# A third row group in seven block products, and the row groups in another order

## The reference

```python
h = relu(layernorm(x))                                   # 5120 x 64
u = par_u[0] * par_u[1] * (diag_u[:, None] * h[:2048] @ W_u) + h[:2048]
i = par_i[0] * par_i[1] * (diag_i[:, None] * h[2048:] @ W_i) + h[2048:]
e = concatenate([u, i])                                  # 5120 x 64
g = adj @ (adj.T @ e)                                    # two products with the large matrix
out = x + layernorm(g) * ln_gamma + ln_beta + h
```

## Time and profile before

| what | before |
|---|---|
| median of 3 runs | 371.39 us (371.16 to 372.5) |
| the profiled execution | 371.32 us |
| its span, first to last instruction | 369.5 us |
| TensorE busy | 98% of the span |
| VectorE, GpSimd, ScalarE busy | 71%, 43%, 20% |
| mean granted TensorE clock | 0.997 of full speed |
| HBM read | 131.55 MB, 360 GB/s over the span |

### The profile page before, as it was taken

The page is one execution under the profiler, slowest core; times in us unless marked ns, Lnnn a source line. Parts: engine busy times, 40 slices in busy tenths (PEclk is TensorE's granted clock), DMA queues, the critical chain, the costliest instruction groups (busy, mean ns, idle before and its releaser), DMA issues.

```text
span 369.5 us, 10865 instructions
## 1 busy us (share of the span) xinstructions
PE 360.3 (98%) x4776; PEld 151.7 (41%) x4776; DVE 263.0 (71%) x282; ACT 74.3 (20%) x213; POOL 159.6 (43%) x94
## 2 busy tenths in 40 slices
PE   7998999999999999999999999999999999999994
PEld 4664454543323443443334334334433343344432
DVE  5999994999061969395677839694956768385266
ACT  5863022010050004001300500040023005002422
POOL 2023060020019902970793199049607931990036
PEclk9999999999999999999999999999999999999998
DMA  8999999999999978989898989889898989853933
GB/s 311 422 419 415 418 426 419 419 419 402 403 380 411 363 291 331 427 343 411 323 429 331 419 326 425 338 318 421 349 409 326 427 339 413 325 247 132 426 130 142
DMA packets 19897, 133.22 MB, mean 361 GB/s; under 512 B 2209, under 2 KB 2977, under 8 KB 4001
## 3 DMA queue, kind: packets, MB, share of 16 engines
q1 hardware_dynamic: 19440, 132.22, 88.1%
q10 hardware_dynamic: 432, 0.66, 0.5%
HBM read 131.55 MB, written 1.31 MB: 360 GB/s over the span
## 4 chain that ended last, share of the span: by engine, by line
PE 87%; DMA 7%; POOL 2%; SPq 2%; DVE 1%; issue 0%; ACT 0%; DVEq 0%; POOLq 0%
PE h_acc L887 36%; PE t_acc L918 24%; DMA natural<-adj_rows 7%; PE x_acc L955 7%; PE h_acc L975 7%; PE t_acc L856 5%; PE t_acc L955 5%; PE h_acc L870 2%; POOL xs L424 1%; SPq L289 1%; POOL sums L420 1%; PE t_acc L993 1%; DVE xs L795 0%; SPq L286 0%; DVE sums L784 0%
## 5 line engine op out<-in xcount | busy, mean ns | idle before, releaser
L599 DVE STREAM_TRANSPOSE strips<-natural 128x2048 f32<-128x2048 f32 x76 | 169.0, 2279 | 48.2 <-PE h_acc L887 48.0
L887 PE MATMUL h_acc<-strips,tokens 32*64 32x512 f32 x2432 | 133.5, 589 | 0.1
L918 PE MATMUL t_acc<-natural,e 128*32 128x512 f32 x832 | 92.3, 592 | 0.1
L887 PEld LDWEIGHTS h_acc<-strips,tokens 32*64 32x64 f32 x2432 | 53.3, 132 | 79.4 <-issue 74.3
L399 POOL TENSOR_TENSOR sums<-natural 128x1024 f32<-128x1024 f32 x14 | 33.3, 2381 | 113.4 <-DMA natural<-adj_rows 113.4
L918 PEld LDWEIGHTS t_acc<-natural,e 128*32 128x32 f32 x832 | 27.4, 110 | 59.4 <-issue 58.2
L955 PE MATMUL x_acc<-sums,forms 128*32 128x256 f32 x280 | 41.1, 380 | 0.0
L856 PE MATMUL t_acc<-natural,e 128*64 128x256 f32 x320 | 36.5, 382 | 1.4 <-DMA natural<-adj_rows 1.1
L489 ACT COPY smalls<-x_acc 32x256 f32<-32x256 f32 x7 | 2.6, 365 | 170.1 <-PE t_acc L955 170.1
L479 ACT COPY tokens<-tokens 32x384 f32<-32x384 f32 (+2 forms) x60 | 24.2, 403 | 51.6 <-DVE tokens L623 30.9
L407 POOL TENSOR_TENSOR sums<-natural,sums 128x1024 f32<-128x1024 f32 x14 | 33.3, 2379 | 1.1
(11 more groups left out here) (97 smaller groups left out, 299.8 us busy)
## 6 DMA issues: line engine op xcount, KB each, us to landing
natural<-adj_rows SPq DMA_DIRECT2D x100, 1024.0 KB, 7.9
cols<-adj_cols SPq DMA_DIRECT2D x20, 1024.0 KB, 11.6
natural<-adj_last SPq DMA_DIRECT2D x4, 1024.0 KB, 10.8
out<-xs SPq DMA_DIRECT2D x4, 256.0 KB, 2.0
xs<-x ACTq DMA_DIRECT2D x2, 256.0 KB, 5.3
xs<-x SPq DMA_DIRECT2D x2, 256.0 KB, 7.7
out<-xs SPq DMA_DIRECT2D x2, 128.0 KB, 2.0
smalls<-small SPq DMA_DIRECT2D x1, 150.0 KB, 3.6
```

The costliest lines, as they stand in the source:

```text
L599: nc.vector.transpose(strips[:, a, :, m].rearrange("p c t i -> p t c i"), natural[:, a, m].rearrange("p t (c j) -> p t c j", j=Q)).then_in ...
L887: last = nc.tensor.matmul(h_acc[D * s:D * (s + 1), q], t[part, a, b, u, :], rows, start=(isinstance(g, int) and g == 0 and b == 0 and u == 0),
L918: last = nc.tensor.matmul(t_acc[lane, pair_bank(half)].rearrange("p (a w) -> p a w", a=2), e[:, GT * m + 2 * k + s, Q * v:Q * (v + 1)], na ...
```

## The change

Row groups 4, 1 and 2 of pairs 3 to 9 are now in seven block products; 0 and 3 stay plain. `ORDER` becomes (0, 4, 1, 2, 3): `first_early` does 0 plain and 4 summed, `first_rest` does 1 and 2 summed and 3 plain. GpSimd has twelve adds for a pair in place of eight, in the order 4, 1, 2. There is no more room for the new sums, so the sums of row group 2 take the three places of those of row group 4, and one of them takes the second half of the slot of row group 4 of the even panel. That slot is therefore loaded in two halves: the first as soon as row group 4 of the pair before is multiplied, the second (semaphore `s_late`) only when row group 2 of the pair before is. The transposes of a pair are taken in another order, seven of the eight before the work on `t`; `u` and `v` move to another PSUM tile, and `v` is made before the first `turn_t`.

```diff
-ORDER = (0, 1, 4, 2, 3)
-EARLY = 2
-TURNS = (0, 1, 3, 2)
-BEHIND = 2
-SUMMED = (4, 3)
+ORDER = (0, 4, 1, 2, 3)
+TURNS = ((0, 0), (0, 1), (0, 2), (1, 0), (1, 1), (0, 3), (1, 2), (1, 3))
+BEHIND = 1
+SUMMED = (4, 1, 2)
+SHARED = 2
-SCRATCH = 2048
+SCRATCH = 1024
...
-        u, sixth_rest, _, v = (x_acc[Q * lane:Q * (lane + 1), WIDE:2 * WIDE] for lane in range(QUADRANTS))
+        sixth_rest = x_acc[Q:2 * Q, WIDE:2 * WIDE]
+        u, v = (t_acc[0:Q, 1, WIDE * n:WIDE * (n + 1)] for n in range(2))
...
+            def load_half(g, s, loaded):
+                sp.dma_start(block_of(0, TURNED, s).rearrange("p k c -> p (k c)"),
+                             adj_rows[g, TURNED, :, HALF * WIDE * s:HALF * WIDE * (s + 1)]).then_inc(loaded, 16)
...
             for g in range(PAIRED + 2, PANELS, 2):
+                sp.wait_ge(s_first, firsts_pair(g // 2 - 1, TURNED))
+                load_half(g, 0, s_natural[0][TURNED])
+                load_natural(g + 1, TURNED)
                 for a in range(2):
-                    for m in range(EARLY):
-                        refill(g + a, m)
-                for m in (4, 3, 2):
-                    for a in range(2):
-                        refill(g + a, m)
+                    refill(g + a, 0)
+                for a in range(2):
+                    refill(g + a, 1)
+                sp.wait_ge(s_first, firsts_pair(g // 2 - 1, SHARED))
+                load_half(g, 1, s_late)
+                for a in range(2):
+                    refill(g + a, 2)
+                refill(g, 3)
                 for a in range(2):
                     refill_cols(g - 2 + a)
+                refill(g + 1, 3)
...
                 for m in SUMMED:
                     for a in range(2):
                         pool.wait_ge(s_natural[a][m], 16 * (half + 1))
-                    pool.wait_ge(s_first, firsts_pair(half - 1, m))
+                    if m == SHARED:
+                        pool.wait_ge(s_first, firsts_pair(half, TURNED))
+                    else:
+                        pool.wait_ge(s_first, firsts_pair(half - 1, SHARED if m == TURNED else m))
...
+                    if m == TURNED:
+                        pool.wait_ge(s_late, 16 * (half - FIRST_HALF))
                     pool.wait_ge(s_sums, sums_done(half, m, 3))
                     nc.gpsimd.tensor_tensor(sum_of(m, 3), block_of(0, m, 1), sum_of(m, 1),
                                             ALU.subtract).then_inc(s_sums, 1)
...
+                dve.wait_ge(s_v, 2 * (half - FIRST_HALF) - 1)
+                nc.vector.tensor_tensor(v, first_v, uv, ALU.add).then_inc(s_v, 1)
                 dve.wait_ge(s_t_left, left + 3)
                 turn_t(2 * half, 0, slice(0, WIDE))
-                dve.wait_ge(s_v, 2 * (half - FIRST_HALF) - 1)
-                nc.vector.tensor_tensor(v, first_v, uv, ALU.add).then_inc(s_v, 1)
...
             def first_rest(half):
-                first_summed(half, 4)
-                first_plain(half, 2)
-                first_summed(half, 3)
+                first_summed(half, 1)
+                first_summed(half, 2)
+                first_plain(half, 3)

             def first_early(half):
-                for m in range(EARLY):
-                    first_plain(half, m)
+                first_plain(half, 0)
+                if not isinstance(half, int):
+                    pe.wait_ge(s_v, 2 * (half - FIRST_HALF - 1))
+                pe.wait_ge(s_late, 16 * (half - FIRST_HALF))
+                first_summed(half, TURNED)
...
             for m in ORDER:
                 first_plain(FIRST_HALF, m)
             second_loaded(PAIRED - 1, 1, PAIRED // 2 - 1)
+            pe.wait_ge(s_forms, FORMS * len(SUMMED))
             first_early(FIRST_HALF + 1)
-            pe.wait_ge(s_forms, 4 * len(SUMMED))
```

More of the change, by code:

```diff
@@ L34 @@
 LAST_HALF = LAST // 2
-ORDER = (0, 1, 4, 2, 3)
-EARLY = 2
-TURNS = (0, 1, 3, 2)
-BEHIND = 2
-SUMMED = (4, 3)
+ORDER = (0, 4, 1, 2, 3)
[3 more added lines that the diff above has]
+SHARED = 2
 FORMS = 4
-SUMS = 4 * len(SUMMED)
+SUMS = FORMS * len(SUMMED)
 LEFT = 5
@@ L122, in gnn_layer @@
         s_natural = [[sem(f"s_natural{a}{m}") for m in range(GROUPS)] for a in range(2)]
+        s_late = sem("s_late")
         s_cols = [sem(f"s_cols{a}") for a in range(2)]
@@ L192, in sums_done, with turns_of, turned_all @@
         def sums_done(half, m, n=4):
-            return SUMS * (half - FIRST_HALF - 1) + 4 * SUMMED.index(m) + n
+            return SUMS * (half - FIRST_HALF - 1) + FORMS * SUMMED.index(m) + n
         def turned_count(g, m):
-            return TURNED * g + (TURNS.index(m) if g >= PAIRED else m) + 1
+            if g < PAIRED:
+                return TURNED * g + m + 1
+            return TURNED * (g - g % 2) + turns_of(g - g % 2).index((g % 2, m)) + 1
+        def turns_of(g):
+            return [(a, m) for a, m in TURNS if g + a < LAST]
+        def turned_all(g, a):
+            if isinstance(g, int) and g < PAIRED:
+                return TURNED * (g + 1)
+            turns = turns_of(g) if isinstance(g, int) and g == LAST - 1 else TURNS
+            return TURNED * (g - a) + 1 + max(n for n, turn in enumerate(turns) if turn[0] == a)
         def block_of(a, m, s):
@@ L204, in sum_of @@
         def sum_of(m, n):
-            if m == TURNED:
-                return block_of(1, m, 0) if n == 2 else sums[:, (0, 1, None, 2)[n]]
-            return sums[:, FORMS - 1 + n]
+            if m == TURNED and n == 2:
+                return block_of(1, TURNED, 0)
+            if m == SHARED and n == 2:
+                return block_of(0, TURNED, 1)
+            return sums[:, FORMS - 1 + n if m == 1 else (0, 1, None, 2)[n]]
         def form_of(m, n):
@@ L382, in _ @@
             pool.wait_ge(s_e_centred, GROUPS)
-            parts = e[:, GT * 3:GT * 5].rearrange("p (m k s) (v d) -> p m k s v d", m=2, s=2, v=2)
+            parts = e.rearrange("p (m k s) (v d) -> p m k s v d", m=GROUPS, s=2, v=2)
             for m in SUMMED:
-                low, high = (parts[:, m - 3, :, s] for s in range(2))
+                low, high = (parts[:, m, :, s] for s in range(2))
                 nc.gpsimd.tensor_tensor(form_of(m, 0), low[:, :, 1], low[:, :, 0], ALU.subtract).then_inc(s_forms, 1)
@@ L678, in turn_pair @@
             def turn_pair(half, t_ready):
-                turn_first(half)
-                for m in TURNS[:-BEHIND]:
-                    turn_strips(2 * half + 1, 1, half, m)
+                for a, m in TURNS[:-BEHIND]:
+                    turn_strips(2 * half + a, a, half, m)
                 t_ready(half)
[L684 to L689, removed]
+                for a, m in TURNS[-BEHIND:]:
+                    turn_strips(2 * half + a, a, half, m)
             def keep_t_plain(half):
@@ L756, in _ @@
                 turn_pair(half, keep_t_pair)
-            turn_first(LAST_HALF)
+            for a, m in turns_of(LAST - 1):
+                turn_strips(LAST - 1, a, LAST_HALF, m)
             keep_t_pair(LAST_HALF)
@@ L877, in second_strips @@
             def second_strips(g, a, blocks=range(BLOCKS)):
-                pe.wait_ge(s_strips, TURNED * (g + 1))
+                pe.wait_ge(s_strips, turned_all(g, a))
                 pe.wait_ge(s_t, g + 1)
```

## The result

The changed kernel takes 388.4 us (median of 4 runs, 387.69 to 390.67) against 371.49 us: a ratio of 1.046, 95% interval 1.0422 to 1.0497. The prediction was 380.5 us, range 377.0 to 384.0: the sign was right, the size was not.

A forecast was written before the change was run, and what follows sets the result against it. TensorE's back-to-back instructions were taken as the bound. From 371.32 us: - 2.9 gain + 3.6 first stall + 3.7 second + 1.8 tail + 0.4 `v` + 0.7 late half + 1.85 clock = 380.5 us; range 377.0 to 384.0.

The forecast's parts named there:

- the 0.4 us for `v`: In the tail, v made ahead of the first `turn_t` makes `t` of the even panel later, costing 0.4 us.
- what a seventh product saves: Turning one plain row group of a pair into a summed one saves 0.41 us, 2.9 us over 7 pairs.
- The first stall: At the start, TensorE waits from 89.40 to 92.99 us for group 4 of panel 5, now asked for second: 3.6 us.
- I take one fall, 1.85: TensorE's clock drops to half speed after one of the two start stalls, costing 1.85 us; bounds 0 and 3.7.
- one late pass, 0.7: In the loop, the late half load makes TensorE wait 0.7 us in one of six passes; bounds 0 and 4.2.
- the second stall: At the start, at 112.36 us, TensorE waits 3.7 us for GpSimd's fourth add, itself behind the late half load.
- the tail's wait for group 2: In the tail fewer strips stand ahead of `first_rest(9)`, so TensorE waits 1.8 us for the sums of group 2.
- a fall for both stalls: Rival: both start stalls cost the clock, 382.3 us in all; chance 0.15.
- known as a bound: One long step between load landings at the start would make the second stall 4.9 us in place of 3.7.
- 0.5 us of slack: In the loop the late half load lands by 27.45, and GpSimd's fourth add needs it by 28.0.
- a sign of being wrong: A loop pass longer than 33.8 us would show the prediction wrong; passes of 33.4 were expected.

The follow-up runs named there:

- The run with filled waits: The changed kernel with matmuls nobody reads added in the two waits at the start and the tail's wait: 385.0 us, ratio 1.0361.
- the kernel before with a late load: The kernel before with panel 5's row groups loaded in the order 0, 2, 3, 4, 1, so group 1 lands last: 376.31 us, ratio 1.0135.
- the last run: Changed kernel with loads reordered and v moved back, its tail now multiplying plain group 3 between summed groups 1 and 2: 368.98 us, ratio 0.9935.

## Why the prediction was right or wrong

Right: the places. The gap at 90 us (3.6 forecast, 3.53 measured), a second gap that GpSimd's fourth add ends after a wait for the late half, the wait for the sums of group 2 in the tail, the 0.4 us for `v`. Right too what a seventh product saves: 0.41 a pass, shown by the passes of 33.42 us once the waits are gone. The first stall is shown from both sides: taken out of the changed kernel it gives back 4.7 us with its half clock, put alone into the kernel before it costs 3.4 to 6.2.

Wrong: four sizes, all on one side. In the profiled execution:

| step of the prediction | forecast | measured | more |
|---|---|---|---|
| the clock: "I take one fall, 1.85" | 1.85 | 1.6 + 2.4 + 1.7 = 5.7 | 3.85 |
| the late half in the loop: "one late pass, 0.7" | 0.7 | 204.1 - 6 x 33.41 = 3.6 | 2.9 |
| the second stall: 3.7 | 3.7 | 5.9 | 2.2 |
| the tail's wait for group 2: 1.8 | 1.8 | 2.3 | 0.5 |

With these 380.5 becomes 390.0, and TensorE began pair 2 0.5 us later (86.40 against 85.90): 390.5 of the 390.67 us. The median of the four executions is 2.3 us lower; their mean clock is 0.980 to 0.986, the profiled one's 0.981.

- The clock is the step that failed most. Its term was sized by one fall for two stalls, and the tail's wait was not counted at all. All three waits were followed by half clock: four products in 15.6 for 14.0 us (1.6), group 4 summed in 5.5 for 3.0 to 3.2 (2.4), group 2 summed in the tail in 4.7 for 3.0 (1.7). The run with filled waits shows it as a cause: clock 1.00, 3.4 us less by the medians. The rule cited from the Trainium skill, "TensorE: Matmul & The Clock Gate", section "Why this matters for your kernels", that an idle gap between bursts of matmuls takes the clock back, would have given a nearer term, a fall for both stalls. The trace agrees with it for both (half clock behind 3.53 and 5.91 us), but the profiled execution of the kernel before with a late load has a gap of 3.48 us and no fall.
- The second stall was the right mechanism with too quick a queue: six MB were put at 4.7 + 12.5 = 17.2 us and took 19.0, with one long step of 4.0 us. That step was known as a bound (4.9 us for the stall) and was taken for the rare case. The queue is 1.8 of the 2.2 us. The first stall's half clock is almost no part of it: it delayed the release of the loads and TensorE's asking nearly alike (98.9 for 96.5, and 114.6 for 112.4). The remaining 0.4 us are hand-overs.
- The loop had 0.5 us of slack by the prediction's own working, and such a slack is no cover. The late half landed 9.1 us after its issue in the first pass, where 27.45 - 20.1 = 7.35 was forecast, and TensorE waited 1.43 us; waits of 0.2 to 0.5 follow in three later passes. The load ahead of it landed as forecast (152.2 is 26.2 after the pass began); what was mis-sized is the half MB's own step, 1.25 in the forecast and 3.0 here. Even a pass without a visible wait took 33.62 to 33.67: the sums came just as TensorE asked (191.4), and the first 18 matmuls of group 4 took 1.27 us (191.47), where the earlier trace rows have 1.07. The first pass and the last, 35.05 and 34.1, are clearly longer than 33.8, which the prediction itself had named as a sign of being wrong. Ordering the half load earlier brought 33.42.
- The range failed because each upper bound stood alone in its rival. The late terms go together: the second stall and the late half hang on the same queue of loads, and the clock fell behind three of the waits. The bounds given (3.7 for the clock, 4.2 for the loop, 4.9 for the second stall) in one sum make 371.32 - 2.9 + 3.6 + 4.9 + 1.8 + 0.4 + 4.2 + 3.7 = 387.0, and the measured loss of the clock lies above its bound.

Not settled: why some steps between landings take 4.0 us and not 2.5 (at the start it is the same load, group 1 of panel 7, in the changed kernel, in the run with panel 5 reordered and in the last run, with 4.0 to 4.2 us), and why in the loop of the changed kernel the half MB lands from 1.4 to 3.0 us behind the load ahead of it, where 1.25 was reckoned. No run varied this.

## What to carry to other kernels

A change that makes the bounding engine's work shorter is worth nothing until each wait that it adds is checked at the places where the pipeline is not in its steady state: here 0.41 us a pass was gained, and the waits, with the half clock behind them, cost more than six times the sum of it. When the order of use changes, the order of the loads has to follow, first of all for a load that lands just in time (0.09 us of waiting in the chain was the sign). A wait of TensorE's can cost more than its length, and bounds of terms that depend on one queue have to be added, not taken one at a time.

## What the runs showed of the hardware

A wait of 2.3 us in the tail, with dense work before it, was followed by half clock (mean 0.62 over the next 4.5 us), while one of 3.48 us in the kernel before with a late load was not (1.00). Work whose result is thrown away kept the clock at 1.00 where it filled the waits. GpSimd's adds of 128 x 1024 took 2.36 to 2.38 us on average whether it worked for 43% of the span (before) or for 62% (the last run).
